# A recommender's lookups, feature products and two layers on one core: products two tiles ahead of layer 1, in quarters, and three more tables looked up by matmul

## The reference, cut to what matters

```
e = jnp.stack([tbl_0[ids[:, 0]], ..., tbl_25[ids[:, 25]]], axis=1)
combined = jnp.concatenate([dense[:, None, :], e], axis=1)            # 512 x 27 x 128
interactions = jnp.einsum('bnd,bmd->bnm', combined, combined)
z = jnp.concatenate([dense, interactions[:, triu_i, triu_j]], axis=1)
h = jnp.concatenate([z, dense], axis=1)
h = jnp.maximum(h @ W_top1 + b_top1, 0.0)                             # 607 -> 512
h = jnp.maximum(h @ W_top2 + b_top2, 0.0)                             # 512 -> 256
y = h @ W_top3                                                        # 256 -> 1
```

## Time and profile before

| | us |
|---|---|
| median of 3 runs | 155.07 (153.86 to 156.51) |
| the profiled execution | 153.22 |
| its span, first to last instruction | 151.4 |
| PE busy | 108.7 |
| GpSimd busy | 72.5 |
| VectorE busy | 60.5 |
| ScalarE busy | 53.1 |

### The profile page before, as it was taken

How to read it: one execution, slowest core, us unless ns; L and a number is a source line. 1 busy time by engine, 2 the same in 40 slices (tenths; PEclk the granted TensorE clock), 3 DMA queues, 4 the chain that set the end, 5 groups by cost and what they waited for, 6 DMA issues and landing times.

```text
span 151.4 us, 3509 instructions
## 1 busy us (share of the span) xinstructions
PE 108.7 (72%) x1506; PEld 88.2 (58%) x1506; DVE 60.5 (40%) x147; ACT 53.1 (35%) x112; POOL 72.5 (48%) x64
## 2 busy tenths in 40 slices
PE   6689999995999099942011101296999899889993
PEld 2257787884878087831100000285998889778891
DVE  2499999999899960000000000005105104010410
ACT  3567779788278711020000000011305202341242
POOL 1688889998878887777777774000000000000000
PEclk9999999999999857996555555558999999999999
DMA  5999965676489612122211211000000000000000
GB/s 135 265 254 283 268 209 170 152 192 202 143 232 322 257 41 52 52 52 52 52 52 52 52 52 52 0 4 0 4 4 4 4 4 4 0 0 4 4 4 1
DMA packets 6255, 13.96 MB, mean 92 GB/s; under 512 B 1792, under 2 KB 3460, under 8 KB 6112
## 3 DMA queue, kind: packets, MB, share of 16 engines
q1 hardware_dynamic: 4294, 9.56, 21.5%
q0 software_dynamic: 1792, 3.67, 9.5%
q10 hardware_dynamic: 154, 0.51, 1.0%
HBM read 13.73 MB, written 0.00 MB: 91 GB/s over the span
## 4 chain that ended last, share of the span: by engine, by line
PE 41%; POOL 24%; issue 24%; DMA 6%; ACT 2%; DVE 1%
POOL rows_sb L274 24%; PE ps_gram L328 14%; PE ps_a L369 8%; PE ps_a L293 7%; PE ps_h L383 4%; DMA rows_sb<-tbl,ids_sb 4%; PE ps_rows L307 3%; DMA ids_sb<-ids 2%; PE ps_a L358 2%; PE ps_z L344 1%; ACT zt L583 1%; ACT xt L564 1%; DVE zz L503 1%; PE ps_h L397 1%; PE ps_h L410 1%
## 5 line engine op out<-in xcount | busy, mean ns | idle before, releaser
L274 POOL DMA_INDIRECT rows_sb<-tbl,ids_sb x56 | 71.8, 1283 | 20.0 <-issue 16.8
L293 PE MATMUL ps_a<-onehot,part_sb 125*128 125x512 f32 x196 | 50.5, 413 | 1.9 <-ACT part_sb L538 1.5
L293 PEld LDWEIGHTS ps_a<-onehot,part_sb 125*128 125x128 f32 x196 | 37.7, 198 | 12.4 <-ACT part_sb L538 2.0
L328 PE MATMUL ps_gram<-xt 128*27 128x27 f32 x1024 | 20.9, 230 | 29.5 <-issue 28.1
L328 PEld LDWEIGHTS ps_gram<-xt 128*27 128x27 f32 x1024 | 18.0, 149 | 32.9 <-issue 30.8
L483 DVE TENSOR_SCALAR onehot<-idrow,row_id 125x512 fp32r<-125x512 int16 x86 | 35.2, 482 | 4.4 <-DMA idrow<-ids_by_table 3.7
L503 DVE STREAM_TRANSPOSE zz<-ps_gram 128x864 f32<-128x864 f32 x3 | 3.2, 1083 | 57.3 <-PE ps_gram L328 57.3
L564 ACT COPY xt<-ps_rows 128x256 f32<-128x256 f32 (+2 forms) x32 | 9.3, 353 | 39.6 <-PE ps_rows L307 39.6
L487 DVE TENSOR_TENSOR part_sb<-table_sb,part_sb 125x1024 fp32r<-125x1024 f32 (+1 forms) x12 | 14.9, 1240 | 0.0
L557 ACT COPY xt<-ps_a 128x512 f32<-128x512 f32 x12 | 7.0, 587 | 19.3 <-PE ps_a L293 14.2
L538 ACT CAST part_sb<-table_sb 125x1024 fp32r<-125x1024 f32 (+1 forms) x12 | 12.8, 1070 | 2.6 <-DMA table_sb<-tbl 2.6
(11 more groups left out here) (35 smaller groups left out, 36.2 us busy)
## 6 DMA issues: line engine op xcount, KB each, us to landing
table_sb<-tbl SPq DMA_DIRECT2D x10, 448.0 KB
idrow<-ids_by_table SPq DMA_DIRECT2D x12, 128.0 KB
w_sb<-w SPq DMA_DIRECT2D x1, 1280.0 KB, 8.5
rows_sb<-tbl,ids_sb POOLq DMA_INDIRECT x56
table_sb<-tbl SPq DMA_DIRECT2D x1, 560.0 KB
table_sb<-tbl SPq DMA_DIRECT2D x10, 52.0 KB
w_sb<-w SPq DMA_DIRECT2D x1, 512.0 KB
table_sb<-tbl ACTq DMA_DIRECT2D x1, 448.0 KB
```

Of the source, the lines that this page charges most:

```text
L274: pool.indirect_dma_start(rows_sb[:, t % ROWS_RING, GATHERED.index(f), :], None, tables[f], bass.IndirectOffsetOnAxis(ids_sb[:, t, f:f + 1 ...
L293: last = pe.matmul(ps_a[:, h % 2, :], parts_sb[part][:, w, c * D:(c + 1) * D], onehot[:, w, c, :], start=(part == HIGH and c == 0), stop=( ...
L328: last = pe.matmul(ps_gram[j * NPAD:j * NPAD + N, half, s * N:(s + 1) * N], x, x, start=True, stop=True)
```

## The change

Fifteen tables are looked up by matmul instead of twelve (0, 1, 5 and 7, of 1250 rows each, take the place of 0 alone), eleven are gathered: 44 gathers in 12 groups. The lookups are in ten units of one or two tables; VectorE compares both tables of a unit in one instruction of 1024 columns, and makes the LOW parts in halves, at written-out places between compares. A lookup runs as four quarters: first half of the chunks HIGH, then LOW, second half HIGH, then LOW. The last two lookups run in two pieces of 256 samples; the first pieces, which tiles 0 and 1 need, stand at their place, the second pieces go between the products of tiles 0 and 1. Products are in quarters, two tiles ahead of layer 1: a quarter of `gram(t + 2)` after each quarter of tile t's pair part. Odd tiles' layer 1 uses the banks of `ps_rows`. The last tile has no order of its own any more: VectorE packs its whole triangle, and `layer2_last` waits for both halves. Gathers wait for lookups: six are free, then three more with each finished lookup; their ring holds two tiles. Index rows have a ring of three units, and a table's slot is free again once its LOW part is made. The first table is loaded by two issuing queues, its id row first on ScalarE's. The arrays of the later stages lie in the table ring's memory. `RUN` is 2.

```diff
-RUN = 4
+RUN = 2
-ONEHOT_TABLES = [4, 10, 11, 17, 19, 20, 24, 25, 3, 8, 14, 0]
-CHUNKS = [8] * 11 + [10]
+ONEHOT_TABLES = [4, 10, 11, 0, 17, 19, 1, 20, 24, 5, 25, 3, 7, 8, 14]
+CHUNKS = [8] * 3 + ([10] + [8] * 2) * 4
+UNITS = [[0], [1, 2], [3], [4, 5], [6], [7, 8], [9], [10, 11], [12], [13, 14]]
+UNIT_RING = 2
+IDROW_RING = 3
-ROWS_RING = 3
+ROWS_RING = 2
+SPLIT = 2
+COLUMNS = [[(0, B)]] * (NOH - SPLIT) + [[(0, B // 2), (B // 2, B)]] * SPLIT
+def place(h, piece):
+    return h + SPLIT * piece
-GROUP_SIZES = [4, 4, 3, 3]
+GROUP_SIZES = [4, 4, 3]
-AFTER_LOOKUP = [[], [], [0], [], [1], [2], [3], [], [4], [5], [], [6]]
-IN_GRAM = [[7], []]
-BEFORE_GRAM = [[8], [11], [13]]
-AT_END = [[9, 10], [12]]
-LAST = [14, 15]
+AFTER_LOOKUP = [[], [], [], [0], [1], [2], [3], [4], [5], [], [6], [7], [8], [9], []]
+BETWEEN_PRODUCTS = [10, 11]
-WARM_UP = 10
+WARM_UP = 13
+GATHERS_PER_LOOKUP = 3
+GATHERS_AHEAD = 6
...
+        def h1_block(t, m):
+            banks = ps_rows if t % 2 else ps_a
+            return banks[:, m // 2, (m % 2) * P:(m % 2 + 1) * P]
...
                 if h >= TABLE_RING:
-                    sp.wait_ge(lookup_done, h - TABLE_RING + 1)
+                    sp.wait_ge(part_ready[LOW], 2 * (h - TABLE_RING + 1))
...
                 for n in features:
                     f = n - 1
+                    if issued >= GATHERS_AHEAD and (issued - GATHERS_AHEAD) % GATHERS_PER_LOOKUP == 0:
+                        pool.wait_ge(lookup_done, (issued - GATHERS_AHEAD) // GATHERS_PER_LOOKUP + 1)
+                    issued += 1
...
+            def lookup(h, piece=0, quarters=range(4)):
+                w, chunks, u = h % WORK_RING, CHUNKS[h], UNIT_OF[h]
+                member = h - UNITS[u][0]
+                a, b = COLUMNS[h][piece]
...
+                for half in range(2):
+                    for part in PARTS:
+                        if 2 * half + part not in quarters:
+                            continue
...
+                        for c in range(half * chunks // 2, (half + 1) * chunks // 2):
...
+                            last = pe.matmul(ps_a[:, place(h, piece) % 2, a:b], parts_sb[part][:, w, c * D:(c + 1) * D],
+                                             unit_onehot(u, c)[:, member, a:b], start=(part == HIGH and c == 0),
+                                             stop=(part == LOW and c == chunks - 1))
...
+            lookup(NOH - 2, 1, [0, 1])
+            gram(0, 0)
+            lookup(NOH - 2, 1, [2])
+            gram(0, 1)
+            lookup(NOH - 2, 1, [3])
+            gram(0, 2)
+            lookup(NOH - 1, 1, [0])
+            gram(0, 3)
+            lookup(NOH - 1, 1, [1])
+            gram(1, 0)
+            lookup(NOH - 1, 1, [2])
+            gram(1, 1)
+            lookup(NOH - 1, 1, [3])
+            gram(1, 2)
+            turn_group(BETWEEN_PRODUCTS[0])
+            gram(1, 3)
             for k in range(2):
-                layer1_pairs(0, k)
+                layer1_dense(0, k)
+            turn_z(0)
+            turn_group(BETWEEN_PRODUCTS[1])
+            for k in range(2):
+                layer1_dense(1, k)
+
             for t in range(TILES - 2):
...
+                for m in range(M1):
+                    layer1_pairs(t, m)
+                    gram(t + 2, m)
+                turn_z(t + 1)
+                layer2(t)
                 for k in range(2):
...
+                    layer1_dense(t + 2, k)
+            for m in range(M1):
+                layer1_pairs(TILES - 2, m)
+            turn_z(TILES - 1)
+            layer2(TILES - 2)
+            for m in range(M1):
+                layer1_pairs(TILES - 1, m)
             layer3(range(TILES - 1))
...
             layer2_last()
-            layer3([t])
+            layer3([TILES - 1])
...
+            def compare(u):
+                members, w = UNITS[u], u % IDROW_RING
+                n = len(members)
...
+                for c in range(COMPARED[u]):
+                    for h, half in LOW_BEFORE[u].get(c, []):
+                        make_low(h, half)
+                    dve.tensor_scalar(unit_onehot(u, c), idrow[0:VP, w, 0:n, :],
                                       row_id[0:VP, first + c:first + c + 1], None, ALU.is_equal).then_inc(onehot_ready, 1)
```

More of the change, by code:

```diff
@@ L323, in gram @@
                         pe.wait_ge(blocks_turned, t)
-                for s in range(SPB):
+                for s in range(first, first + SPQ):
                     for j in range(P // NPAD):
@@ L341, in turn_z, with layer1_dense @@
                 if t:
                     pe.wait_ge(z_copied, t)
-                for c in chunks:
-                    last = pe.transpose(z_bank(t, c)[:, c * P:(c + 1) * P], z[:, c * P:(c + 1) * P], ident)
+                for c in range(ZC):
+                    last = pe.transpose(ps_z[:, 0, c * P:(c + 1) * P], z[:, c * P:(c + 1) * P], ident)
                 last.then_inc(z_turned, 1)
-            def layer1_dense(t):
-                if t == 0:
+            def layer1_dense(t, k):
+                if k == 0 and t == 0:
@@ L352, in layer1_dense @@
                     pe.wait_ge(w1d_summed, 1)
[L353 to L358, removed]
+                    pe.wait_ge(lookup_copied, PIECES)
+                elif k == 0 and t == 1:
+                    pe.wait_ge(group_copied, len(GROUPS))
+                elif t >= 2:
+                    pe.wait_ge(h1_high_ready if k else h1_low_ready, t - 1)
@@ L359, in layer1_dense, with layer1_pairs @@
+                for m in range(2 * k, 2 * k + 2):
+                    pe.matmul(h1_block(t, m), w1d[:, m * P:(m + 1) * P],
                               dense_sb[:, t * P:(t + 1) * P], start=(m % 2 == 0), stop=False, skip_group_check=True)
-            def layer1_pairs(t, k, chunks=range(ZC)):
-                if k == 0:
+            def layer1_pairs(t, m):
+                if m == 0:
                     if t == 0:
                         pe.wait_ge(w1_landed, 16)
[L366 to L371, removed]
-                    last.then_inc(h1_done, 1)
@@ L374, in layer2 @@
[L374 to L381, removed]
+                    pe.wait_ge(z_copied, t + 1)
+                for c in range(ZC):
+                    last = pe.matmul(h1_block(t, m), w1_sb[:, c, m * P:(m + 1) * P],
+                                     zt[:, t % 2, c, :], start=False, stop=(c == ZC - 1), skip_group_check=True)
@@ L402, in layer3 @@
+                pe.wait_ge(h1_high_ready, t + 1)
+                for m in range(M2):
+                    for k in range(M1):
+                        last = pe.matmul(h2_block(t, m), w2_sb[:, k, m * P:(m + 1) * P], h1[:, t % 2, k, :],
+                                         start=(k == 0), stop=(k == M1 - 1))
+                    last.then_inc(h2_done, 1)
             def layer3(tiles):
@@ new lines, in make_low @@
+            def make_low(h, half):
+                s, w, middle = h % TABLE_RING, h % WORK_RING, CHUNKS[h] // 2 * D
+                columns = slice(middle, CHUNKS[h] * D) if half else slice(0, middle)
+                dve.wait_ge(part_ready[HIGH], rounded(h, half))
+                dve.tensor_tensor(parts_sb[LOW][:, w, columns], table_sb[0:VP, s, columns],
+                                  parts_sb[HIGH][:, w, columns].bitcast(F32), ALU.subtract).then_inc(part_ready[LOW], 1)
+            for u in range(len(UNITS)):
+                compare(u)
@@ L492, in _ @@
+            for h, half in LOW_AT_END:
+                make_low(h, half)
+            dve.wait_ge(part_ready[LOW], 2 * NOH)
             dve.memset(z[:, ZUSED:], 0.0)
@@ L494, in _, with pack @@
             dve.tensor_tensor(w1d[:, :], w1_sb[:, ZC, :], w1_sb[:, ZC + 1, :], ALU.add).then_inc(w1d_summed, 1)
-            for t in range(TILES):
+            def pack(t):
                 dve.wait_ge(gram_done, t + 1)
```

316 lines of the change are left out of this document (141 added, 175 removed).

## The result

The changed kernel takes 126.73 us (median of 4 runs, 124.9 to 127.47), the kernel before beside it 154.47 us (153.81 to 156.51): ratio 0.8149, 95% interval 0.7997 to 0.83. The forecast was 137, so the sign is right and the size is 10 us off. The profiled execution took 127.47 us; its span is 125.4 us, so 2.1 lie around it. Executions of one kernel fall into a faster and a slower group: medians here are over all of them, ratios over the faster group alone, so that a ratio need not be the quotient of two medians.

What follows compares the result with a forecast made beforehand. The hole was the largest single item; PE and VectorE shared the lookups' bound. With gathers leading afterwards, first product at 82.3 plus 51.3 made a span of 133.6; 1.8 and 1.85 more gave 137 us, range 125 to 150 (0.84).

Steps and rivals of the forecast that it cites:

- The hole: Near-idle PE at the kernel before's first products, 65.33 to 97.97 us: 31.6 us lost, said to end with the gathers.
- Rival C: First dense products or that place in PE's instructions, not gathers, cause the stall; it stays: 169 us, chance 0.14.
- So the gathers lead: Lookup stage: gathers at 1.97 us keep PE until group 9's rows land at 76.7; first product at 82.3.
- rival A: Lookup stage: gathers below 1.64 us each don't bind; first product 70.8, about 126 us; chance 0.15.
- the case that had 0.60: Whole kernel: the forecast, including D and a short rest of the hole, 131 to 145 us; chance 0.60.
- Rival B: Lookup stage: gathers get dearer beside pair compares, 2.4 us each, 144.5 us in all; chance 0.09, up to 150.
- From the first product on: Products and layers to the end: work 43.2, waits 2.5, end 5.6 us, together 51.3 us.
- RUN 2 instead of 4: Products: halved stride of PE's feature reads, shorter ScalarE write runs; priced at zero, 2 us either way.
- The 0.9 for group 11's copy: After the first product: 0.9 us of PE waiting left for the copy of the gathered rows of group 11.
- The pair compare: VectorE in lookups: one compare over 1024 columns costs 0.675 us, between bounds of 0.408 and 0.816.
- D: VectorE's pair compare saves nothing, 0.816 us each: 139 us; its chance is counted within the forecast's 0.60.
- the pace: Gathers held to three per lookup, six ahead: costs nothing as long as gathers stay slower than lookups.

Runs made afterwards that it cites:

- the last kernel above: The kernel before with the gathers of tiles 2 and 3 left out, run on chip E: 124.73 us, ratio 0.8024 to the full kernel before.

## Why the prediction was right in sign and 10 us too high

*The hole.* "So the hole ends with the gathers": it goes with them. On chip E their absence alone gives 0.8024 of the time, and the whole change gives 0.8087. Rival C (the hole belongs to the first products, or to that place in PE's instructions) is refuted: the last kernel above has both the products and the place, and no hole. By the rule of the Trainium skill set beside C (SBUF — State Buffer, Who interferes with whom) PE never waits on another engine's port, and a DMA contends with no compute engine; where rule and measurement differ, the measurement stands, for chip E. What the gathers do to PE is not shown: no operand and no semaphore is on record as late, only issue. The hole is on three chips of five. That it goes with the gathers was tried on E; on A and C only its end, 4.9 us behind the last gather, speaks for it. Whether gathers beside products suffice on such a chip wasn't tried, as both kernels with added gathers fell on chips without the hole.

*What the rest of the change is worth.* The changed kernel with eleven gathers more takes 1.0104 (1.0045 to 1.0162) of the kernel before on chip B, with its weights loaded late 1.0166, and on D its lowest time is 122.48 against 119.45. More lookups and earlier products thus buy nothing where there is no hole, and cost about 1% there; the 28 us of chip A are the hole (31.6 forecast), less what the change loses elsewhere. The unedited changed kernel was not run on B or D, so that its own number there is open.

*The step that failed: "So the gathers lead".* It priced 44 gathers at 1.97 us and had them keep PE until group 9's rows landed at 76.7. They took 1.51, and in the whole list of waits PE waits for gathered rows not once, which the prediction had named as the sign of rival A. Rival A had the point from which it decides, 1.64, the first product at 70.8 and a time of about 126; its chance was 0.15, and the case that had 0.60 did not come. The price 1.97 was a mean of unlike gathers: of the first 25, beside whole subtractions and single compares, two took 3.60 us, three 2.02 and the others 1.10 to 1.92. In the changed kernel a gather at 22.16 takes 1.01 us in the middle of seven pair compares. The timeline of VectorE and GpSimd in the changed kernel, a gather beside pair compares and one beside subtractions:

```profile
19.63 4.72 DVE L547 TENSOR_SCALAR onehot<-idrow,row_id 125x1024 fp32r<-125x1024 int16 x7
...
22.16 1.01 POOL L335 DMA_INDIRECT rows_sb<-tbl,ids_sb  x1 [0.30 <-issue]
...
30.36 1.55 DVE L556 TENSOR_TENSOR part_sb<-table_sb,part_sb 125x640 fp32r<-125x640 f32 x2
30.47 2.65 POOL L335 DMA_INDIRECT rows_sb<-tbl,ids_sb  x1 [0.30 <-issue]
```

The same in the kernel before, a gather that lies wholly within seven single compares:

```profile
13.60 2.86 DVE L483 TENSOR_SCALAR onehot<-idrow,row_id 125x512 fp32r<-125x512 int16 x7
...
14.91 1.28 POOL L274 DMA_INDIRECT rows_sb<-tbl,ids_sb  x1 [0.31 <-issue]
```

Subtractions hold gathers up most; single compares do so a little (1.28 for 1.01), pair compares hardly. Both edits, halved subtractions and paired compares, can thus have made gathers cheaper. How much each gave is not shown: no run changed one of them alone. Rival B (gathers dearer) fell with it.

*What kept PE instead.* First product 74.25 and not A's 70.8: 2.21 us of the 3.45 is the wait for VectorE's LOW part. The rest is the lower clock behind it (0.50 from 69.4 to 70.1 us, 0.69 in the mean from there to 74.25): four transposes held PE for 0.70 us instead of 0.36, and the 24 half-width matmuls took 4.16 us, where they took 3.03 on chip B. VectorE was late because it and ScalarE had been signalled late. The timelines of ScalarE and VectorE in the changed kernel, columns as before:

```profile
57.30 0.66 ACT L634 COPY xt<-ps_a 128x512 f32<-128x512 f32 x1 [3.59 <-remote]
...
62.33 0.67 ACT L634 COPY xt<-ps_a 128x512 f32<-128x512 f32 x1 [2.56 <-remote]
...
62.41 4.73 DVE L547 TENSOR_SCALAR onehot<-idrow,row_id 125x1024 fp32r<-125x1024 int16 x7 [1.71 <-remote]
```

The matmuls that the two copies wait for had ended at 54.18 and 58.27, 3.1 and 4.1 us earlier by PE's rows. ScalarE, VectorE and GpSimd (62.33, 62.41, 62.57) all three go on at once after the second, so it is the signal that was late and not one of them. Without late signals, on chips B and D, the first product starts at 68.5 to 69.3, with them, on C and E, at 71.90 and 73.11. No forecast had this.

*From the first product on.* Forecast 51.3, measured 125.4 - 74.25 = 51.15: luck, by errors that cancel. Sixteen quarters of products at 0.68 for 0.99 gave back 4.9 us. "RUN 2 instead of 4 ... I take zero, 2 us either way" is the term: the stride alone is worth 5.3 us of PE (0.33 by 16, the run with RUN 4), outside its own bound. Here the rule was to be had: the Trainium skill (Advanced Engine Details and Errata, SBUF Cachelines) gives SBUF lines of 16 bytes and wants two hits on each. With a stride of four floats each feature has a line of its own, with two floats two share one; the runs agree, 1.02 us against 0.69 for 64 records. Against it stand 4.2 us of issue stops that nothing in the sum stood for, and 1.0 of half-width matmuls: in quarters of four, between products, they take 0.67 a quarter for the 0.50 priced, though 0.125 each was right for runs of 24. The 0.9 for group 11's copy was 0.59.

*The rest of the 10 us.* The first product accounts for 8.0 us. Another 2.3 us is no work of the kernel: the forecast put 3.65 us between the span of a profiled execution and the median of the runs (1.8 and 1.85), and here it was 1.33.

*Right as forecast.* The pair compare, 4.72/7 = 0.674 for 0.675, so that D (the pair compare saves nothing) fell; the pace, that costs nothing; no run of near-empty slices.

## What to carry to other kernels

When PE stands with idle time put down to issue beside GpSimd's indirect DMAs, leave those DMAs out in one run before anything is rebuilt: it gives the size of the stall without touching PE's order. Run both kernels on more than one chip: a change that took the time to 0.81 on one gained nothing on another. Price a gather by what VectorE runs beside it in the new order, not by the mean of the old, and put the elements of a small strided matmul operand 8 bytes apart rather than 16.

## What the runs showed of the hardware that was not expected

*The hole is there on some chips only.* With one and the same kernel before: 154.5, 159.0 and 159.0 us on A, C and E; 122.9 and 124.8 on B and D. The late signals keep to the same chips: in the changed kernel ScalarE's copies have waits of 2.1 to 4.5 us with no releaser on the core's record on A, C and E, and none in its variants on B and D. The profiles of the kernel before have no such wait on any chip. A common cause is possible; none was found.

*The hole has a beat of its own.* PE's last records in it start at 99.93, 100.63 and 101.33 on chip C, 0.70 us apart, and 96.57, 97.27 and 97.97 on A; late in the hole the longer gaps are 1.40, 2.10 or 2.80 from start to start, multiples of the same 0.70. The gathers are 1.25 apart. So PE isn't released by each gather as it ends; what beats at 0.70 is not shown.

*PE's stops in dense small matmuls follow packets of instructions.* The DMA view of the changed kernel from 74 to 86 us, 40 slices of 0.3 us:

```profile
GB/s 0 0 0 55 0 0 0 0 0 0 0 0 0 0 55 0 0 0 0 0 0 0 0 0 0 0 55 0 0 0 0 0 0 0 0 0 0 0 55 0
...
q8 instruction: 4, 0.07, 2.1%
```

Only four packets of instructions move, 0.07 MB in all, in the slices that start at 74.9, 78.2, 81.8 and 85.4. The stops end at 80.67, 84.34 and 87.63, 2.2 to 2.5 us after the last three; after the first there is none. Two more packets come at 92.0 and 95.9, and the other two stops end at 94.64 and 98.37, 2.6 and 2.5 us behind them. In the kernel with longer runs of products on chip C the stop of 2.23 us ends 2.6 us behind its packet (93.7). So the end of a stop keeps its distance to the packet, and its length depends on how soon before that end PE has nothing left to issue. The Trainium skill (Runtime: NRT & Kernel Launch, Instruction fetch mechanics) calls the cost of going from one fetched block of instructions to the next mostly hidden; here the stops are 4.2 us of 125. That they are waits for those packets is read from their order in time, and no run took the fetches away. The hole of the kernel before is another thing: no such packet moved in it between 60 and 90 us.
